# Moving the softmax division of a local-attention kernel from ScalarE to VectorE

## The chip, the cores and the metric

The kernel runs on one core of a Trainium2 chip. The metric is the device time of one execution in microseconds, from the first to the last instruction with the small launch share around them; lower is better. The engines are PE (TensorE, matrix products and transposes), ACT (ScalarE), DVE (VectorE), POOL (GpSimd) and SP (SyncE, which issues the DMAs here). Each has a queue of its own and works it off strictly in order; they meet at semaphores.

## The reference

The input is `x` of 2 sequences x 2048 tokens x 512 features and a context of 2 x 154 tokens. All arithmetic is fp32. Cut to what matters:

```
x = x + cross_attention(layernorm(x), ctx, ctx)          # 16 heads
h = layernorm(x)
for l in range(2):                                        # local attention + gated FFN
    qkv = shift_token(h) @ wqkv[l]                        # 512 -> 3 x 512, 8 heads of 64
    q, k = rotary_xpos(l2norm(q) * qs, l2norm(k) * ks)
    sim  = (8 * q) @ k.T                                  # query block of 256, keys of it and the block before
    sim  = where(mask, -max, sim)                         # query i sees keys i-256 .. i
    attn = softmax(sim)                                   # exp(sim - max) / sum
    h    = h + (attn @ v) @ wo[l]
    z    = layernorm(shift_token(h)) * g + b
    a, g = split(z @ w1 + b1);  h = h + (a * gelu(g)) @ w2 + b2
out = x + h
```

## The kernel before

The 4096 tokens are 32 tiles of 128 (`NT = 32`). The phases follow one another: context and cross attention, then twice (for `l` 0 and 1) an attention phase and an FFN phase. Every fp32 product is made of three fp32r products (`split_matmul`, L46 to L48), of a rounded high part, which ACT writes (`hi_...`), and a remainder, which DVE writes (`lo_...`).

`attention_phase` is the function that the change touches. Each engine runs a hand-written order over the tiles `t`, pipelined so that projections run for tile `t + 2`, rotary and key work for `t + 1`, and softmax and values for `t`. A tile has 8 heads in two halves of four (`LANES = 4`). For one head: PE writes scores to PSUM (`scores`, L1246), DVE adds the mask and finds the maximum (`masked`, L1477, out `neg_s`, `neg_m`), ACT takes the exponential with a running sum (`exponent`, L1365, out `prob`, `sm`), DVE inverts the sums of two heads at a time (`recip`, L1486, out `rc`), and ACT multiplies `prob` in place by `rc` (`divide`, L1374). PE then transposes `prob` (`transpose_p`, L1258) into the PSUM bank of the head four further on, so it also waits until `masked` has read that bank. ACT and DVE split the transposed probabilities (`hi_p` L1380, `lo_p` L1491), PE multiplies with `v` (`values`), ACT and DVE split the result (`hi_o` L1390, `lo_o` L1501), and PE applies `wo` (`output`). A full tile sees 384 keys, the first two tiles of each sequence 128 and 256.

Beside it go the norms of q and k. ACT squares the projection (`squares`, L1338), DVE sums it and clamps it (`norms`, L1446 and L1448), POOL takes the root as a power (L1156, `rn`), DVE scales (`normalise`, L1454, `qk`), and POOL applies the rotary tables in four instructions: one with the cosines (L1162), two halves with the sines (L1168), and their sum (L1172, `m`). `a = 0` is q and `a = 1` is k. PE transposes `m` (L1227). `lo_v` (L1461), `lo_h` (L1440) and `residual` (L1510) are further DVE steps of one instruction each; `project(t + 2, 0)` on PE waits for `lo_h(t + 2)`, and `hi_v` (L1344) on ACT precedes `lo_v`.

At the end of the phase DVE also prepares the first FFN group: `ffn_moments` (L1614 to L1620) and `ffn_normalise` (L1632), with a root on POOL between them (L1626).

Of the kernel before, what the change touches and what calls it, by code (L numbers as in the profile page):

```python
# [9 lines left out]
ACT = mybir.ActivationFunctionType  # L10
# [939 lines left out]
def attention_sems(sem):  # L950

    s = {n: [sem(f"a_{n}{u}") for u in range(4)] for n in ("ld_h", "ld_rot", "ld_y", "st")}
    for n in ("ld_small", "k_copy", "dv_own", "pe_h", "ac_h", "dv_h", "pe_qkv", "ac_sq", "dv_ssq", "pl_rn", "dv_norm",
              "pl_tab", "pl_m1", "pl_m2", "pl_rot", "ac_v", "dv_v", "pe_r", "ac_r", "dv_r", "pe_s", "dv_s", "ac_exp", "dv_rc", "ac_p",
              "pe_t", "ac_t", "dv_t", "pe_o", "ac_o", "dv_o", "pe_w", "dv_y"):
        s[n] = sem(f"a_{n}")
    s["w_ld"], s["w_hi"], s["w_lo"] = [sem(f"w_attn_ld{k}") for k in range(SLOTS["w_attn"])], sem("w_attn_hi"), sem("w_attn_lo")
    return s
# [16 lines left out]
def attention_phase(nc, io, ps, ident, s, neg_half, l, h_in, y_in, w, dram, ahead):  # L975
    LH = NT * HEADS

    with ExitStack() as st:
# [38 lines left out]
        def nth(total, n):  # L1017

            return l * total + max(n, 0)
# [5 lines left out]
        def seen(t):  # L1025
            return slice(first_block(t) * P, KEYS)
# [31 lines left out]
        with nc.Block() as block:  # L1058
# [131 lines left out]
            def _(e):  # L1190
# [60 lines left out]

                def transpose_p(t, h):
                    n = HEADS * t + h
                    e.wait_ge(s["ac_p"], nth(LH, n + 1))

                    e.wait_ge(s["dv_s"], nth(LH, min(n + LANES + 1, LH)))
                    for k in range(first_block(t), 3):
                        last = e.transpose(ps[:, bank_head(h), k * P:(k + 1) * P], prob[:, n % 4, k * P:(k + 1) * P], ident[:])  # L1258
                    last.then_inc(s["pe_t"], 1)
# [16 lines left out]
                def output(t):  # L1276
                    if t < 0:
                        return
                    if t == 0:
                        e.wait_ge(w_lo, w.done(w.count))  # L1280
                    e.wait_ge(s["dv_o"], nth(2 * NT, 2 * t + 2))

                    e.wait_ge(s["dv_r"], nth(2 * NT, min(2 * t + 6, 2 * NT)))
                    for c in range(DC):
                        last = split_matmul(e, ps[:, bank_y(t), :], [x[:, t % 2, c, :] for x in oT], [x[:, c, :] for x in wo], c == 0, c == DC - 1)
                    last.then_inc(s["pe_w"], 1)
# [10 lines left out]
                for t in range(NT):  # L1297
                    if t:
                        scores(t, 1)
                    project(t + 1, 2)  # L1300
                    transpose_h(t + 2)
                    if t == 0:
                        scores(t, 1)
                    for h in range(LANES):
                        transpose_p(t, h)
                    transpose_qk(t + 1)
                    project(t + 2, 0)
                    for h in range(LANES):
                        values(t, h)

                    scores(t + 1, 0)
                    project(t + 2, 1)
                    if t == NT - 1:
                        output(t - 1)
                    for h in range(LANES, HEADS):
                        transpose_p(t, h)
                    if t < NT - 1:
                        output(t - 1)
                    for h in range(LANES, HEADS):
                        values(t, h)  # L1320
                output(NT - 1)
# [2 lines left out]
            def _(e):  # L1324
# [34 lines left out]
                def exponent(t, h):  # L1359
                    if t < NT:  # L1360
                        n = HEADS * t + h
                        m = n % 4
                        e.wait_ge(s["dv_s"], nth(LH, n + 1))
                        e.wait_ge(s["pe_t"], nth(LH, n - 3))
                        e.activation(prob[:, m, seen(t)], neg_s[:, m, seen(t)], ACT.Exp, bias=neg_m[:, m:m + 1], scale=-1.0,  # L1365
                                     accum_out=sm[:, m:m + 1]).then_inc(s["ac_exp"], 1)

                def divide(t, p):

                    if t < NT:  # L1370
                        n = HEADS * t + 2 * p
                        e.wait_ge(s["dv_rc"], nth(LH // 2, n // 2 + 1))
                        for m in (n % 4, n % 4 + 1):
                            e.activation(prob[:, m, seen(t)], prob[:, m, seen(t)], ACT.Copy, scale=rc[:, m:m + 1]).then_inc(s["ac_p"], 1)  # L1374

                def hi_p(t, h):
                    n = HEADS * t + h
# [24 lines left out]
                squares(1, 1)  # L1402
                for h in range(LANES):
                    exponent(0, h)
                divide(0, 0)
                divide(0, 1)
                for t in range(NT):
                    hi_o(t - 1, 1)
                    hi_v(t + 1)
                    hi_h(t + 2)  # L1410
                    for h in range(LANES):
                        hi_p(t, h)
                    hi_qk(t + 1)
                    for h in range(LANES, HEADS):
                        exponent(t, h)
                    divide(t, 2)
                    squares(t + 2, 0)
                    divide(t, 3)

                    hi_o(t, 0)  # L1420
                    squares(t + 2, 1)
                    for h in range(LANES, HEADS):
                        hi_p(t, h)
                    for h in range(LANES):
                        exponent(t + 1, h)
                    divide(t + 1, 0)
                    divide(t + 1, 1)
                hi_o(NT - 1, 1)

            @block.vector  # L1430
            def _(e):
# [18 lines left out]
                def normalise(t, a):  # L1450
                    if t < NT:
                        e.wait_ge(s["pl_rn"], nth(2 * NT, 2 * t + a + 1))
                        e.wait_ge(s["pl_rot"], nth(2 * NT, 2 * t + a - 1))
                        e.tensor_tensor(token_major_heads(qk[:, a, :]), token_major_heads(ps[:, bank_qkv(t, a), :]),  # L1454
                                        rn[:, a, :].rearrange("p (h o) -> p h o", o=1).to_broadcast([P, HEADS, DH]),
                                        ALU.mult).then_inc(s["dv_norm"], 1)
# [7 lines left out]
                def lo_qk(t):  # L1464
                    if t < NT:
                        for a in range(2):
                            e.wait_ge(s["ac_r"], nth(2 * NT, 2 * t + a + 1))
                            hi, out = ((qT[x][:, t % 2] if a == 0 else kT[x][:, :, 2 + t % 4, :]) for x in range(2))
                            e.tensor_tensor(out, ps[:, bank_r(t, a), :].rearrange("p (c t) -> p c t", c=DC), hi.bitcast(F32),
                                            ALU.subtract).then_inc(s["dv_r"], 1)  # L1470
# [7 lines left out]
                                               scalar=3.0e38, op0=ALU.add, op1=ALU.min, accum_out=neg_m[:, n % 4:n % 4 + 1]  # L1478
                                               ).then_inc(s["dv_s"], 1)

                def recip(t, p):

                    if t < NT:
                        n = HEADS * t + 2 * p
                        e.wait_ge(s["ac_exp"], nth(LH, n + 2))
                        e.reciprocal(rc[:, n % 4:n % 4 + 2], sm[:, n % 4:n % 4 + 2]).then_inc(s["dv_rc"], 1)  # L1486

                def lo_p(t, h):
                    n = HEADS * t + h
# [36 lines left out]
                norms(1, 1)  # L1526
                for h in range(LANES):
                    masked(0, h)
                recip(0, 0)
                recip(0, 1)  # L1530
                normalise(1, 1)
                for t in range(NT):
                    for h in range(LANES, HEADS):
                        masked(t, h)
                    lo_o(t - 1, 1)
                    residual(t - 2)
                    lo_v(t + 1)
                    lo_h(t + 2)
                    for h in range(LANES):
                        lo_p(t, h)  # L1540
                    lo_qk(t + 1)
                    if t == NT - 1:
                        ffn_normalise(e, ahead["s"], ahead["t"], l, 0)
                    recip(t, 2)
                    recip(t, 3)
                    norms(t + 2, 0)

                    for h in range(LANES):
                        masked(t + 1, h)
                    lo_o(t, 0)  # L1550
                    normalise(t + 2, 0)
                    norms(t + 2, 1)
                    for h in range(LANES, HEADS):
                        lo_p(t, h)
                    recip(t + 1, 0)
                    recip(t + 1, 1)
                    normalise(t + 2, 1)
                    if t == NT - 2:
                        ffn_moments(e, ahead["s"], ahead["t"], l, 0)
                residual(NT - 2)  # L1560
                lo_o(NT - 1, 1)
                residual(NT - 1)
# [443 lines left out]
```

## Time and profile before

| | |
|---|---|
| device time, 3 runs | 3564.11 us median (3563.64 to 3566.64) |
| profiled execution, device time | 3564.11 us |
| its span, first to last instruction | 3562.3 us |
| PE, DVE, ACT, POOL busy | 96%, 55%, 48%, 32% of the span |
| attention phases | about 600 to 1320 us and 2100 to 2820 us of the span |

The busy shares are means over phases that differ. DVE, ACT and POOL are most busy in the two attention phases and much less in the FFN phases; PE is busy nearly throughout. Matmuls are pipelined and overlap in the rows, so the distance between the starts of two of them is less than the duration of one. The same holds for the other engines, where an instruction's row begins a little before the one ahead of it ends.

### The profile page before, as it was taken

The numbers are of one execution on the slowest core, as the hardware profiler recorded it, in microseconds if no ns is written. First come the engines' busy times: TensorE is split into PE (matmuls) and PEld (weight loads), VectorE is DVE, ScalarE is ACT, GpSimd is POOL, SyncE is SP. The second block draws the span as 40 slices with busy tenths as digits, with TensorE's granted clock in tenths as the row PEclk, the third lists the DMA queues.
The fourth block names the chain that finished last, engine by engine and source line by source line (L and its number), as shares of the span: only waits on it lengthen the run. The fifth ranks groups of instructions, "written<-read, shape, count | busy, mean of one in ns | idle before, by whom it ended". The sixth has DMA issues, their size and how long they took to land. (4 is left out here: it accounts for less than half of the span.)

```text
span 3562.3 us, 56374 instructions
## 1 busy us (share of the span) xinstructions
PE 3412.7 (96%) x20560; PEld 2797.1 (79%) x20560; DVE 1955.5 (55%) x4484; ACT 1702.7 (48%) x4490; POOL 1133.0 (32%) x1008
## 2 busy tenths in 40 slices
PE   7999996999999989999999979999999899999999
PEld 5666675888888877888888858888888778888887
DVE  6888875677777764223323247776777643233322
ACT  5666663677777763111111137777777521111111
POOL 3434433555555520000000035555555121101111
PEclk9999998999999999999999989999999999999999
DMA  4112213111221122111111111112111331111111
GB/s 123 42 46 65 72 42 125 37 60 60 65 67 61 61 87 83 44 44 43 43 44 44 64 65 51 61 61 65 64 60 58 120 100 49 36 46 50 45 37 38
DMA packets 186869, 216.26 MB, mean 61 GB/s; under 512 B 27094, under 2 KB 125654, under 8 KB 186595
## 3 DMA queue, kind: packets, MB, share of 16 engines
q1 hardware_dynamic: 186595, 212.65, 18.6%
q8 instruction: 166, 2.72, 0.3%
q14 instruction: 108, 0.88, 0.1%
HBM read 125.79 MB, written 69.00 MB: 55 GB/s over the span
## 5 line engine op out<-in xcount | busy, mean ns | idle before, releaser
L1917 DVE SCALAR_TENSOR_TENSOR u_full<-banks,b_cols,gate 128x512 f32<-128x512 f32 (+1 forms) x176 | 132.1, 750 | 877.2 <-ACT gate L1875 803.8
L1875 ACT ACTIVATE gate<-banks,b_cols 128x512 f32<-128x512 f32 (+1 forms) x176 | 121.3, 689 | 1008.3 <-PE banks L48 1008.3
L46 PE MATMUL banks<-fxT_h,w_h 128*128 128x512 f32 (+1 forms) x1408 | 556.7, 395 | 2.6 <-DVE w_l L1901 2.4
L48 PE MATMUL banks<-fxT_h,w_l 128*128 128x512 f32 (+1 forms) x1408 | 556.9, 395 | 0.0
L47 PE MATMUL banks<-fxT_l,w_h 128*128 128x512 f32 (+1 forms) x1408 | 555.9, 395 | 0.0
L1770 POOL TENSOR_TENSOR sums<-sums,b_rows 128x512 f32<-128x512 f32 x64 | 85.5, 1368 | 878.7 <-DMA sums<-z_rows 878.7
L46 PE MATMUL banks<-wqkv_h,hT_h 128*128 128x512 f32 x768 | 325.7, 424 | 15.8 <-DVE wqkv_l L1435 14.4
L46 PEld LDWEIGHTS banks<-fxT_h,w_h 128*128 128x128 f32 (+1 forms) x1408 | 260.2, 185 | 70.3 <-DVE w_l L1901 3.7
L48 PEld LDWEIGHTS banks<-fxT_h,w_l 128*128 128x128 f32 (+1 forms) x1408 | 260.8, 185 | 67.4
L47 PEld LDWEIGHTS banks<-fxT_l,w_h 128*128 128x128 f32 (+1 forms) x1408 | 260.5, 185 | 67.1
L48 PE MATMUL banks<-wqkv_h,hT_l 128*128 128x512 f32 x768 | 305.0, 397 | 0.0
L47 PE MATMUL banks<-wqkv_l,hT_h 128*128 128x512 f32 x768 | 304.9, 397 | 0.0
L1365 ACT ACTIVATE prob<-neg_s,neg_m 128x384 f32<-128x384 f32 (+2 forms) x512 | 302.5, 629 | 3.4 <-DVE neg_m L1477 3.4
L1374 ACT ACTIVATE prob<-prob,rc 128x384 f32<-128x384 f32 (+2 forms) x512 | 273.3, 613 | 7.5 <-DVE rc L1486 7.5
L46 PE MATMUL banks<-pT_h,v_h 128*64 128x128 f32 x1440 | 265.1, 223 | 11.3 <-DVE pT_l L1491 11.3
L48 PE MATMUL banks<-pT_h,v_l 128*64 128x128 f32 x1440 | 264.7, 222 | 0.0
L47 PE MATMUL banks<-pT_l,v_h 128*64 128x128 f32 x1440 | 264.6, 222 | 0.0
L1477 DVE CUSTOM_DVE_ANT_0 neg_s<-banks,mask 128x384 f32<-128x384 f32 (+2 forms) x512 | 242.2, 529 | 24.9 <-PE banks L1246 24.2
L1156 POOL TENSOR_TENSOR rn<-ssq,neg_half 128x8 f32<-128x8 f32 x128 | 211.8, 1655 | 130.8 <-DVE ssq L1448 130.6
L46 PE MATMUL banks<-w_h,u_h 128*128 128x512 f32 x640 | 251.8, 393 | 0.5 <-DVE u_l L1922 0.5
L47 PE MATMUL banks<-w_l,u_h 128*128 128x512 f32 x640 | 250.6, 392 | 0.0
L48 PE MATMUL banks<-w_h,u_l 128*128 128x512 f32 x640 | 249.0, 389 | 0.0
(190 smaller groups left out, 8095.3 us busy)
## 6 DMA issues: line engine op xcount, KB each, us to landing
y_rows<-sums SPq DMA_DIRECT2D x16, 1024.0 KB
sums<-y_rows SPq DMA_DIRECT2D x64, 256.0 KB, 2.9
z_rows<-sums SPq DMA_DIRECT2D x64, 256.0 KB, 2.0
sums<-z_rows SPq DMA_DIRECT2D x16, 1024.0 KB, 5.6
thirds<-in_w SPq DMA_DIRECT2D x30, 512.0 KB, 4.9
thirds<-in_x SPq DMA_DIRECT2D x8, 1024.0 KB, 6.9
x_rows<-thirds SPq DMA_DIRECT2D x8, 1024.0 KB, 4.3
thirds<-y_rows SPq DMA_DIRECT2D x64, 128.0 KB, 2.8
```

The source lines that it names most:

```text
L46: pe.matmul(out, a_h, b_h, start=start, stop=False)
L47: pe.matmul(out, a_h, b_l, start=False, stop=False)
L48: return pe.matmul(out, a_l, b_h, start=False, stop=stop)
L1156: e.tensor_tensor(rn[:, a, :], ssq[:, a, :], neg_half[:, 0:HEADS], ALU.pow).then_inc(s["pl_rn"], 1)
L1365: e.activation(prob[:, m, seen(t)], neg_s[:, m, seen(t)], ACT.Exp, bias=neg_m[:, m:m + 1], scale=-1.0, accum_out=sm[:, m:m + 1]).then_inc( ...
L1374: e.activation(prob[:, m, seen(t)], prob[:, m, seen(t)], ACT.Copy, scale=rc[:, m:m + 1]).then_inc(s["ac_p"], 1)
L1477: e.tensor_tensor_reduce(out=neg_s[:, n % 4, seen(t)], in0=ps[:, bank_head(h), seen(t)], in1=mask[:, seen(t)], scale=-1.0, scalar=3.0e38, ...
L1770: e.tensor_tensor(res[:, tt, :], res[:, tt, :], b2[:], ALU.add).then_inc(s["pl_b2" if ends else "pl_res"], 1)
L1875: e.activation(gate[r, :], ps[r, 2 * (m % 2) + 1, :], ACT.Gelu, bias=b1[r, place[m], 1:2]).then_inc(s["ac_g"], 1)
L1917: e.scalar_tensor_tensor(out=u_full[r, m % 2, :], in0=ps[r, 2 * (m % 2), :], scalar=b1[r, place[m], 0:1], in1=gate[r, :], op0=ALU.add, op1 ...
```

## The change

The multiplication of `prob` by `rc` moves from ACT (`activation` with a scale) to DVE (`tensor_scalar` in place). DVE's `recip` becomes `divide`: the reciprocal, a wait on its own semaphore, and two multiplications. The semaphore `ac_p` becomes `dv_p`, and `exponent` also waits for the division of the same lane's last head. The orders of DVE, ACT and, in the last tile, PE are rewritten: on DVE `lo_o(t - 1, 1)` comes ahead of `masked(t, 4..7)`, `norms(t + 2, 0)` stands between the two divisions of the second half, and `normalise(t + 2, 1)` now stands ahead of the divisions of `t + 1`; on ACT `squares(t + 2, 0)` stands in the middle of the four exponentials; `ffn_moments` and `ffn_normalise` move by about a tile.

```diff
@@ tensor queue @@
-                    e.wait_ge(s["ac_p"], nth(LH, n + 1))
+                    e.wait_ge(s["dv_p"], nth(LH, n + 1))
...
-                    if t == NT - 1:
-                        output(t - 1)
                     for h in range(LANES, HEADS):
                         transpose_p(t, h)
-                    if t < NT - 1:
-                        output(t - 1)
+                    output(t - 1)
@@ scalar queue @@
+                        e.wait_ge(s["dv_p"], nth(LH, n - 3))
...
-                def divide(t, p):
-                    if t < NT:
-                        n = HEADS * t + 2 * p
-                        e.wait_ge(s["dv_rc"], nth(LH // 2, n // 2 + 1))
-                        for m in (n % 4, n % 4 + 1):
-                            e.activation(prob[:, m, seen(t)], prob[:, m, seen(t)], ACT.Copy, scale=rc[:, m:m + 1]).then_inc(s["ac_p"], 1)
...
-                    for h in range(LANES, HEADS):
-                        exponent(t, h)
-                    divide(t, 2)
+                    exponent(t, 4)
+                    exponent(t, 5)
                     squares(t + 2, 0)
-                    divide(t, 3)
+                    exponent(t, 6)
+                    exponent(t, 7)
...
-                    divide(t + 1, 0)
-                    divide(t + 1, 1)
@@ vector queue @@
-                def recip(t, p):
+                def divide(t, p):
                     if t < NT:
                         n = HEADS * t + 2 * p
                         e.wait_ge(s["ac_exp"], nth(LH, n + 2))
                         e.reciprocal(rc[:, n % 4:n % 4 + 2], sm[:, n % 4:n % 4 + 2]).then_inc(s["dv_rc"], 1)
+                        e.wait_ge(s["dv_rc"], nth(LH // 2, n // 2 + 1))
+                        for m in (n % 4, n % 4 + 1):
+                            e.tensor_scalar(prob[:, m, seen(t)], prob[:, m, seen(t)], rc[:, m:m + 1], None, ALU.mult).then_inc(s["dv_p"], 1)
...
                 for t in range(NT):
+                    lo_o(t - 1, 1)
                     for h in range(LANES, HEADS):
                         masked(t, h)
-                    lo_o(t - 1, 1)
                     residual(t - 2)
                     lo_v(t + 1)
                     lo_h(t + 2)
                     for h in range(LANES):
                         lo_p(t, h)
                     lo_qk(t + 1)
+                    divide(t, 2)
+                    norms(t + 2, 0)
+                    divide(t, 3)
                     if t == NT - 1:
-                        ffn_normalise(e, ahead["s"], ahead["t"], l, 0)
-                    recip(t, 2)
-                    recip(t, 3)
-                    norms(t + 2, 0)
-
+                        ffn_moments(e, ahead["s"], ahead["t"], l, 0)
+
+                    lo_o(t, 0)
+                    normalise(t + 2, 0)
                     for h in range(LANES):
                         masked(t + 1, h)
-                    lo_o(t, 0)
-                    normalise(t + 2, 0)
                     norms(t + 2, 1)
                     for h in range(LANES, HEADS):
                         lo_p(t, h)
-                    recip(t + 1, 0)
-                    recip(t + 1, 1)
                     normalise(t + 2, 1)
-                    if t == NT - 2:
-                        ffn_moments(e, ahead["s"], ahead["t"], l, 0)
+                    divide(t + 1, 0)
+                    divide(t + 1, 1)
+                    if t == NT - 1:
+                        ffn_normalise(e, ahead["s"], ahead["t"], l, 0)
```

## Rows read from the trace of the kernel before

**Rows 1.** The page: busy time, share of the span, instructions.
```profile
PE 3412.7 (96%) x20560; PEld 2797.1 (79%) x20560; DVE 1955.5 (55%) x4484; ACT 1702.7 (48%) x4490; POOL 1133.0 (32%) x1008
```

**Rows 2.** Windows, one tile: stretch, PE, PEld, DVE, ACT, POOL busy, clock, DMA.
```profile
819.20:841.42 22.22, 22.22 (x183) 19.33 (x182) 15.95 (x44) 16.25 (x43) 11.94 (x11) 1.00 0.16 49
```

**Rows 3.** Waits of PE in the first attention phase: us, times, longest.
```profile
PE banks L46 <- DVE pT_l L1491: 5.7, 4, 1.7
...
PE banks L1258 <- DVE neg_m L1477: 2.1, 2, 1.6
```

**Rows 4.** Timeline of DVE in that tile: start, us, line, tiles, idle before.
```profile
820.04 0.56 DVE L1477 CUSTOM_DVE_ANT_0 neg_s<-banks,mask 128x384 f32<-128x384 f32 x1 [0.38 <-PE banks L1246]
...
821.95 0.84 DVE L1501 TENSOR_TENSOR oT_l<-banks,oT_h 64x256 fp32r<-64x256 f32 x2
822.83 0.69 DVE L1510 TENSOR_TENSOR sums<-banks,sums 128x512 f32<-128x512 f32 x1
...
824.77 0.68 DVE L1440 TENSOR_TENSOR hT_l<-banks,hT_h 128x512 fp32r<-128x512 f32 x1
825.37 1.94 DVE L1491 TENSOR_TENSOR pT_l<-banks,pT_h 128x384 fp32r<-128x384 f32 x4
...
836.64 0.17 DVE L1448 TENSOR_SCALAR ssq<-ssq 128x8 f32<-128x8 f32 x1
836.72 1.94 DVE L1491 TENSOR_TENSOR pT_l<-banks,pT_h 128x384 fp32r<-128x384 f32 x4
838.63 0.17 DVE L1486 RECIPROCAL rc<-sm 128x2 f32<-128x2 f32 x1
...
841.19 0.69 DVE L1454 TENSOR_TENSOR qk<-banks,rn 128x512 f32<-128x512 f32 x1 [1.21 <-POOL rn L1156]
```

**Rows 5.** Timeline of POOL, from that tile into the next.
```profile
836.66 1.45 POOL L1168 TENSOR_TENSOR m<-qk,rot 128x256 f32<-128x256 f32 x2
...
841.96 1.29 POOL L1162 TENSOR_TENSOR m<-qk,rot 128x512 f32<-128x512 f32 x1 [0.81 <-DVE qk L1454]
843.20 1.44 POOL L1168 TENSOR_TENSOR m<-qk,rot 128x256 f32<-128x256 f32 x2
844.78 1.30 POOL L1172 TENSOR_TENSOR m<-m 128x512 f32<-128x512 f32 x1
```

**Rows 6.** Timeline of PE in that tile.
```profile
825.87 0.48 PE L46 MATMUL banks<-wqkv_h,hT_h 128*128 128x512 f32 x1
...
830.80 0.22 PE L48 MATMUL banks<-pT_h,v_l 128*64 128x128 f32 x1
```

**Rows 7.** Timeline of ACT in that tile.
```profile
831.85 0.80 ACT L1390 ACTIVATE oT_h<-banks 64x256 fp32r<-64x256 f32 x2
```

**Rows 8.** Groups by line and shape: busy us, mean ns, idle before.
```profile
L1477 DVE CUSTOM_DVE_ANT_0 neg_s<-banks,mask 128x384 f32<-128x384 f32 x448 | 223.0, 554 | 20.0 <-PE banks L1246 19.7
...
L1156 POOL TENSOR_TENSOR rn<-ssq,neg_half 128x8 f32<-128x8 f32 x128 | 211.8, 1655 | 130.8 <-DVE ssq L1448 130.6
...
L1632 DVE TENSOR_SCALAR thirds<-thirds,f_mv,f_rs 128x512 f32<-128x512 f32 x64 | 30.6, 543 | 15.9 <-POOL f_rs L1626 15.9
```

**Rows 9.** One line's instructions in one window: ns min/median/max, first start.
```profile
L833 DVE TENSOR_SCALAR xn<-thirds,x_mv,x_rs x1: 1082/1082/1082, 121.7 to 121.7; 128x512 f32<-128x512 f32 x1
```

**Rows 10.** Timelines of POOL and DVE at 121 us and 597 us.
```profile
121.28 1.21 POOL L575 TENSOR_TENSOR x_prob<-x_prob,x_rc 128x616 f32<-128x616 f32 x1 [0.66 <-DVE x_rc L857]
...
597.40 0.76 DVE L1448 TENSOR_SCALAR ssq<-ssq 128x8 f32<-128x8 f32 x1
...
598.68 1.22 DVE L1435 TENSOR_TENSOR wo_l<-thirds,wo_h 128x512 fp32r<-128x512 f32 x1
...
596.86 1.28 POOL L1162 TENSOR_TENSOR m<-qk,rot 128x512 f32<-128x512 f32 x1 [2.20 <-DVE qk L1454]
598.09 1.25 POOL L1168 TENSOR_TENSOR m<-qk,rot 128x256 f32<-128x256 f32 x1
```

**Rows 11.** Timeline of PE at the end of the first attention phase.
```profile
1302.33 1.95 PE L1258 MATMUL banks<-ident,prob 128*128 128x128 f32 x12 [1.55 <-DVE neg_m L1477]
```

More of the change, by code:

```diff
@@ L953, in attention_sems @@
     for n in ("ld_small", "k_copy", "dv_own", "pe_h", "ac_h", "dv_h", "pe_qkv", "ac_sq", "dv_ssq", "pl_rn", "dv_norm",
-              "pl_tab", "pl_m1", "pl_m2", "pl_rot", "ac_v", "dv_v", "pe_r", "ac_r", "dv_r", "pe_s", "dv_s", "ac_exp", "dv_rc", "ac_p",
+              "pl_tab", "pl_m1", "pl_m2", "pl_rot", "ac_v", "dv_v", "pe_r", "ac_r", "dv_r", "pe_s", "dv_s", "ac_exp", "dv_rc", "dv_p",
               "pe_t", "ac_t", "dv_t", "pe_o", "ac_o", "dv_o", "pe_w", "dv_y"):
@@ L1404, in _ @@
                     exponent(0, h)
-                divide(0, 0)
-                divide(0, 1)
                 for t in range(NT):
@@ L1528, in _ @@
                     masked(0, h)
-                recip(0, 0)
-                recip(0, 1)
                 normalise(1, 1)
+                divide(0, 0)
+                divide(0, 1)
                 for t in range(NT):
+                    lo_o(t - 1, 1)
                     for h in range(LANES, HEADS):
                         masked(t, h)
-                    lo_o(t - 1, 1)
                     residual(t - 2)
```

## The prediction

> **What bounds the kernel now.** I read the page first, for the shares of the engines [rows 1]: PE is busy 96% of the span and DVE, ACT and POOL have room on average. The change lies in the two attention phases, so I then took the windows of one tile there [rows 2]. A full tile takes 22.22 us, PE is busy for all of it at a granted clock of 1.00, DVE for 15.95 us and ACT for 16.25 us. The timelines of the next tiles show the same starts plus 22.22 us. So PE sets the pace. Its waits in a whole attention phase are a few at the ends [rows 3]. Taking work off ACT, which waits for PE, can gain nothing in a full tile; the question is whether DVE, with more to do, begins to hold PE up. For that I read the timelines of the four engines in the tile that starts at 819.20 us [rows 4 to 7], and last the groups and the places where DVE and POOL want something at once [rows 8 to 10].
>
> **What the change costs on DVE.** The nearest row to the new multiplication is L1632, the same instruction with 512 columns and two per-partition scalars: 543 ns [rows 8]. If it took one column per cycle of 0.96 GHz, its 512 columns alone would be 533 ns and leave 10 ns for everything else, while 8 columns (L1448) cost 170 ns [rows 4]. So it takes two columns at a time. With 384 columns it is 67 ns shorter, 476 ns, with one scalar too many; from the other side 170 ns plus 188 columns (98 cycles x 2) make about 370 ns. I take 410 ns, and 330 ns from start to start (rows on DVE overlap by 80 ns [rows 4]). A pair also needs its reciprocal and the wait for it, about 190 ns. Eight heads: 8 x 0.33 + 4 x 0.1 = 3.0 us more per tile. 15.95 + 3.0 = 19.0 us, still under 22.22. ACT loses eight instructions, which nobody behind them on the path needed sooner.
>
> **Where it stands in time.** DVE's order now puts the divisions of heads 0 to 3 behind `normalise(t + 2, 1)`, which waits for a root on POOL and in turn starts POOL's four rotary instructions. Behind the divisions stand `lo_o`, four `masked`, `residual`, `lo_v` and `lo_h`, and for `lo_h` PE waits in `project(t + 2, 0)`, which starts at 825.87, 6.67 us into the tile [rows 6]. From the end of the divisions to `lo_h`: 0.87 (`lo_o`, 821.95 to 822.83), 1.91 (`masked`, 820.04 to 821.95), 0.60 and 0.61 for two instructions of 512 columns, 0.68 and a semaphore of 0.05 for `lo_h` [rows 4]: 4.72 us. DVE must be free of divisions at 6.67 - 4.72 = 1.95 us into the next tile, which begins at 841.42.
>
> Without any conflict it is: `normalise` could start at 839.3 (root done), the two pairs follow at 839.9 and take 2 x 0.85 us, until 841.6, which is 0.2 us into the tile. That leaves 1.75 us of cover.
>
> **The conflict with POOL.** DVE's two-column instructions and POOL's instructions exclude each other. At 597.40 the small L1448 meets POOL's L1162 and takes 0.76 us instead of 0.17; it ends at 598.16, and POOL's ended at 598.14 [rows 10]. At 121.7 L833 (512 columns, two scalars, alone 0.54 us) takes 1.082 us and ends at 122.77, 0.28 us behind the end of POOL's instruction at 122.49 [rows 9, 10]. So a DVE instruction that meets a running POOL one ends 0.02 us plus its columns behind it: 0.22 us for 384. A POOL instruction waits likewise: the half with the sines that starts at 598.09 beside a DVE instruction takes 1.25 us, not 0.72, and DVE's next one, at 598.68, waits for it and takes 1.22 us [rows 10]. They alternate; neither gets two turns in a row. POOL's 0.72 us after a wait is 0.58.
>
> Now the chain, with PE on its old times. PE's values end at 831.02 [rows 6], ACT's `hi_o` needs 0.80 [rows 7], `lo_o` on DVE 0.87, so `normalise(t + 2, 0)` starts at 832.76. POOL starts 0.77 us later (841.19 to 841.96) and reaches its sum 2.82 us after that (to 844.78) [rows 4, 5]: the sum runs from 836.35 to 837.65. The clamp L1448 comes at 836.64 as before, in the middle of it, and waits: DVE goes on at 837.59, not 836.72. Four `lo_p` take 1.91, so `normalise(t + 2, 1)` starts at 839.50; the root is ready (837.67 + 1.66 [rows 8] = 839.33). Then:
> - 840.10 reciprocal, 840.29 division 0; POOL's L1162 starts at 840.27 and ends at 841.55; division 0 ends at 841.77.
> - POOL's first half runs then, to 842.35; division 1 ends at 842.57.
> - Reciprocal 842.49, division 2 is issued at 842.68, POOL's second half runs to 843.15; division 2 ends at 843.37.
> - Division 3 is issued at 843.29. POOL's sum is issued 0.14 to 0.15 us after the half before it (843.20 + 1.44 to 844.78 [rows 5]), at 843.30.
>
> This last is a race within 10 ns. If DVE wins, division 3 ends at 843.70, DVE is free at 843.62, 2.20 us into the tile, 0.25 us late. If POOL wins, its sum runs to 844.50, division 3 ends at 844.72, DVE is free at 844.64, 3.22 us in, 1.27 us late. The trace has a like case: at 836.64 L1448 is 0.02 us ahead of POOL's L1168 (836.66) and takes 0.17 us, no wait [rows 4, 5]. So who is issued first wins, and my times put DVE first by a hair. The loop closes through PE (`lo_h`, projection, values, `hi_o`, and the next norms), so a lateness is paid in full in each tile. `masked(t, 7)` before PE's transposes and the divided `prob` itself have more room than `lo_h`.
>
> How many tiles: 448 `masked` of 384 columns are 56 full tiles [rows 8]; the last two of each layer have no projection behind, so 52. 52 x 0.25 = 13 us; 52 x 1.27 = 66 us.
>
> **The moves at the end of the phase.** `ffn_moments` used to stand ahead of `masked(31, 4..7)`, and PE waited 1.55 us there [rows 11]; now it stands behind. Summed the same way, PE's last values start about 1 us earlier in each layer, in spite of PE's transposes no longer having `output(30)` as cover. Gain 2 us in all. `ffn_normalise` ends before the last `residual` either way.
>
> **What a page says.** The Trainium skill (Advanced Engine Details and Errata, VectorE Performance Modes) says that VectorE's second port is shared with GpSimd and that instructions in a two-port mode and GpSimd's block each other. The rows of 121 and 597 us agree, with 0.54 and 0.59 us of waiting. The skill's VectorE: DVE Perf Modes (The TRN2 errata) estimates such an instruction at 58 cycles plus half its columns, 260 ns for 384; the row of 512 columns, 543 ns against the 327 of that rule, does not bear it out. By that estimate the work added would be 2.5 us per tile and the wait for POOL the same.
>
> **The rivals.**
> - DVE loses the race in most tiles: 3564 + 66 - 2 = 3628 us. For it: POOL needs only 10 ns. Against it: the case at 836.64.
> - The waits are covered. Either the instruction takes one column at a time and does not meet POOL, when 8 of 0.47 us ([rows 4], L1491) still end 0.7 us into the tile, or DVE is elsewhere earlier by the 0.25 us that I find it late. Then only the end of the phase counts: 3562 us.
> - It gets worse than one lost race: at 476 ns a division is free 0.07 us later each time, and the tail of a waiting one can be longer by as much. Four of them add 0.28 us to 1.27: 52 x 1.55 = 81 us, 3643 us.
> - Faster. PE's waits for `lo_p` and `masked` in the first phase are 5.7 + 2.1 us [rows 3], some of them behind ACT's exponentials and divisions at the start and end of the sequences. If ACT's relief removes all, in both layers, it is 15.6 us: 3549 us. It decides only if no full tile is late; against it, most of these waits are at the end, where DVE, not ACT, is last [rows 11].
>
> **How the numbers follow.** The profiled execution, 3564.11 us, is also the median, and its span is 1.8 us less; the sum is 3564.1 + 13 - 2 = 3575 us. Chances: this case 0.36, the lost race 0.28, covered 0.19, worse 0.08, faster 0.09. The range leaves out about a tenth on each side: 3559 to 3642 us. My forecast's own range, with the lateness from 0.05 to 0.45 us, is 3565 to 3585. About 0.2%, 7 us, is what a measurement tells from no change. Faster by more: 0.09. Within it: the covered case and the part of mine with a lateness under 0.17 us, 0.26. Slower: 0.65.
>
> **What would show it.** In the profile after: L1374 gone from ACT; about 512 TENSOR_SCALAR rows on DVE, half of them (heads 4 to 7) near 0.41 us and half stretched to 0.5 to 1.5 us beside POOL's rotary rows; L1448 at 1.0 us in one of two cases; a tile of 22.47 us (23.5 if the race is lost), PE's new waits for `hT_l`, or in the worse case also `neg_m` and `v_l`; POOL's halves stretched by up to 0.1 to 0.5 us. The prediction fails if the divisions are not stretched, if `normalise(t + 2, 1)` comes at another time than 20.3 us into the tile, or if PE's wait falls on `prob` itself.

## The result, and the profile after

The changed kernel takes 3669.08 us (median of 4 runs, 3663.69 to 3672.61), the kernel before 3563.88 us in the same rounds (3562.16 to 3566.64). The ratio is 1.0293, with a 95% interval of 1.0275 to 1.0311: 105 us slower. That is 27 us above the upper end of the predicted range.

The page of the kernel after, its line of busy times:

```profile
PE 3486.1 (95%) x20560; PEld 2795.5 (76%) x20560; DVE 2329.7 (64%) x4996; ACT 1511.2 (41%) x3978; POOL 1148.0 (31%) x1008
```

Against [rows 1], ACT is busy for 191 us less and DVE for 374 us more, with 512 more instructions. At the predicted 0.41 us the 512 would be 210 us. The groups by line and shape of the kernel after (busy us, mean ns, idle before) show the rest:

```profile
L1475 DVE TENSOR_SCALAR prob<-prob,rc 128x384 f32<-128x384 f32 x448 | 332.9, 783 | 7.9
...
L1434 DVE TENSOR_SCALAR ssq<-ssq 128x8 f32<-128x8 f32 x128 | 66.9, 523 | 4.4
```

A division takes 783 ns in the mean, nearly twice what it takes alone, and the eight-column clamp, 0.17 us when alone [rows 4], takes 523 ns.

The window of one full tile, in the columns of [rows 2]:

```profile
834.00:857.53 23.53, 23.36 (x182) 19.25 (x181) 21.45 (x52) 13.17 (x34) 11.99 (x12) 1.00 0.15 47
```

The tile has grown from 22.22 to 23.53 us. PE is still busy for nearly all of it at a clock of 1.00, so neither the share of PE nor the clock tells what happened. The timeline of DVE around the start of this tile, with divisions 0 and 2 also on a row of their own:

```profile
829.21 1.02 DVE L1434 TENSOR_SCALAR ssq<-ssq 128x8 f32<-128x8 f32 x1
830.14 1.94 DVE L1480 TENSOR_TENSOR pT_l<-banks,pT_h 128x384 fp32r<-128x384 f32 x4
832.00 0.68 DVE L1440 TENSOR_TENSOR qk<-banks,rn 128x512 f32<-128x512 f32 x1
...
832.79 1.48 DVE L1475 TENSOR_SCALAR prob<-prob,rc 128x384 f32<-128x384 f32 x1
832.79 2.29 DVE L1475 TENSOR_SCALAR prob<-prob,rc 128x384 f32<-128x384 f32 x2
...
835.19 0.70 DVE L1475 TENSOR_SCALAR prob<-prob,rc 128x384 f32<-128x384 f32 x1
835.19 2.13 DVE L1475 TENSOR_SCALAR prob<-prob,rc 128x384 f32<-128x384 f32 x2
837.24 0.84 DVE L1490 TENSOR_TENSOR oT_l<-banks,oT_h 64x256 fp32r<-64x256 f32 x2
```

And POOL's timeline over the same time:

```profile
832.76 1.28 POOL L1162 TENSOR_TENSOR m<-qk,rot 128x512 f32<-128x512 f32 x1 [0.80 <-DVE qk L1440]
834.00 1.67 POOL L1168 TENSOR_TENSOR m<-qk,rot 128x256 f32<-128x256 f32 x2
835.81 1.29 POOL L1172 TENSOR_TENSOR m<-m 128x512 f32<-128x512 f32 x1
```

Read the ends. POOL's L1162 ends at 834.04 and division 0 at 834.27. The four divisions of one tile take 1.48, 0.89, 0.70 and 1.51 us, in turn with POOL's four instructions. POOL's sum starts at 835.81 and ends at 837.10; division 3 starts at 835.81 too and ends 0.22 us behind it, at 837.32. It waited for the whole sum. So DVE is free at 837.24, 3.24 us into the tile.

The timeline of PE:

```profile
838.83 1.96 PE L1258 MATMUL banks<-ident,prob 128*128 128x128 f32 x12
840.86 1.23 PE L1227 MATMUL banks<-ident,m 128*128 128x128 f32 x8
841.96 0.50 PE L46 MATMUL banks<-wqkv_h,hT_h 128*128 128x512 f32 x1
```

`project(t + 2, 0)` starts 7.96 us into the tile (841.96 - 834.00), not 6.67 [rows 6]. The 12 transposes of `prob`, which take 1.47 us in the kernel before, take 1.96. The timeline of PE's weight loads tells why:

```profile
838.79 0.31 PEld L1258 LDWEIGHTS banks<-ident,prob 128*128 128x128 f32 x3 [0.30 <-issue]
839.27 0.31 PEld L1258 LDWEIGHTS banks<-ident,prob 128*128 128x128 f32 x3 [0.16 <-issue]
839.75 0.31 PEld L1258 LDWEIGHTS banks<-ident,prob 128*128 128x128 f32 x3 [0.17 <-issue]
```

They come in threes, one head at a time, 0.48 us apart, which is the pace of DVE's `masked`. PE runs at DVE's pace here, in gaps that the profile lists as "issue" and does not put down to DVE. It goes on like that up to `project(t + 2, 0)`:

```profile
840.83 0.42 PEld L1227 LDWEIGHTS banks<-ident,m 128*128 128x128 f32 x4 [0.29 <-issue]
841.43 0.42 PEld L1227 LDWEIGHTS banks<-ident,m 128*128 128x128 f32 x4 [0.18 <-issue]
841.96 0.19 PEld L46 LDWEIGHTS banks<-wqkv_h,hT_h 128*128 128x128 f32 x1
```

DVE's `residual` ends at 840.71 and PE goes on at 840.83; `lo_v` ends at 841.31, PE goes on at 841.43; `lo_h` ends at 841.91 and `project` starts 0.05 us later. Behind it no step of PE's tile is later by more than these 1.3 us.

**Where the 105 us are.** `lo_v` runs once per tile, 32 times in a phase. Here is that line by source, in each attention phase of the kernel after (ns min/median/max, first and last start):

```profile
L1447 DVE TENSOR_TENSOR v_l<-banks,v_h x32: 680/681/684, 602.8 to 1339.3; 128x512 fp32r<-128x512 f32 x32
...
L1447 DVE TENSOR_TENSOR v_l<-banks,v_h x32: 679/681/692, 2148.9 to 2883.2; 128x512 fp32r<-128x512 f32 x32
```

The same line in the kernel before:

```profile
L1461 DVE TENSOR_TENSOR v_l<-banks,v_h x32: 680/692/693, 604.9 to 1286.9; 128x512 fp32r<-128x512 f32 x32
...
L1461 DVE TENSOR_TENSOR v_l<-banks,v_h x32: 680/692/693, 2096.0 to 2777.4; 128x512 fp32r<-128x512 f32 x32
```

From first to last it is 736.5 us and 734.3 us now, 682.0 and 681.4 before: 107.4 us more. (The two profiled executions differ by 106.5 us over the whole span; the first `lo_v` comes 2.1 us earlier now.) Of the 31 intervals of a phase, three stand at the start of each of its two sequences, in and next to the tiles with one or two key blocks; there the sum over both phases has grown by 30.1 us. They are called the short tiles below. The other 50 intervals have grown by 77.3 us, 1.55 us each: none is under 23.53 us, and the mean is 23.75.

### The profile page after: what moved, and what is told of

It reads as the page before. It is cut to its first block and busy times, and to the rows that moved or that the text cites. A ratio compares the mean times of both kernels' runs of the same rounds, so it can differ in the third digit from the quotient of the medians.

```text
span 3668.8 us, 56374 instructions
## 1 busy us (share of the span) xinstructions
PE 3486.1 (95%) x20560; PEld 2795.5 (76%) x20560; DVE 2329.7 (64%) x4996; ACT 1511.2 (41%) x3978; POOL 1148.0 (31%) x1008
## 5 line engine op out<-in xcount | busy, mean ns | idle before, releaser
L1475 DVE TENSOR_SCALAR prob<-prob,rc 128x384 f32<-128x384 f32 (+2 forms) x512 | 365.7, 755 | 9.1
L1258 PE MATMUL banks<-ident,prob 128*128 128x128 f32 x1440 | 216.8, 282 | 42.4 <-DVE neg_m L1463 39.2
L575 POOL TENSOR_TENSOR x_prob<-x_prob,x_rc 128x616 f32<-128x616 f32 x128 | 155.5, 1215 | 289.9 <-DVE x_rc L857 289.9
```

The source lines that it names most:

```text
L575: e.tensor_tensor(p4, p4, rc[:, (GT * c + tt) % NS, :].rearrange("p (r o) -> p r o", o=1) .to_broadcast([P, QUAD, SC]), ALU.mult).then_inc ...
L1475: e.tensor_scalar(prob[:, m, seen(t)], prob[:, m, seen(t)], rc[:, m:m + 1], None, ALU.mult).then_inc(s["dv_p"], 1)
```

## The experiments

The theories, as the expectations name them, are stated in full there. In short: the order of the divisions behind `normalise(t + 2, 1)` makes them meet POOL's rotary; the rivals are DVE's added work as such, and the new orders without any conflict.

### POOL's rotary taken almost away: e1_small_rotary, e1b_before_small_rotary

```
-  parts = [[token_major_heads(m[:, a, :]) for m in (qk, m1, m2)] ...]
+  parts = [[token_major_heads(m[:, a, :])[:, 0:1, :] for m in (qk, m1, m2)] ...]
```

The rotation of seven of the eight heads is left out, so the result is another one; the number and order of the instructions stay, but for one memset on POOL in each layer.

> The changed kernel with GpSimd's four rotary instructions cut to one head of eight; VectorE's work, order and number of instructions are those of the changed kernel (the rotation of seven heads is left out of the computation). Theory A (VectorE's divisions and its clamp wait for GpSimd's long instructions at the shared port, and that alone makes VectorE late): full tiles fall back to 22.2 us, divisions to about 0.41 us each, time 3555 to 3572 us. Rival B (3 us more of work per tile on VectorE, queued behind normalise, is enough by itself): tiles stay at 23.5 to 23.8 us and the time near 3669 us. Between them, say 3600 to 3640, both have a share.

> The control: the kernel before with the same cut of GpSimd's rotary instructions (rotation of seven heads left out). TensorE sets the pace of full tiles there, so they stay at 22.22 us; the starts of the phases and sequences, where TensorE waits for the rotated keys, get shorter by some us. Theory A and B both: 3545 to 3564 us. The difference between this and the run above is what the division costs on VectorE with the port conflict gone: A says under 10 us, B about 100 us.

Measured: 3544.53 us (ratio 0.994, 0.992 to 0.996) for the kernel after with the cut, 3524.30 us (0.9883, 0.9863 to 0.9903) for the kernel before with it. Both are below the range expected, by 10 and 21 us: the short tiles got shorter than thought, by 33.3 us in the second. The window of a full tile of the first:

```profile
819.20:841.42 22.22, 22.22 (x183) 19.34 (x181) 18.91 (x51) 12.57 (x35) 6.53 (x11) 1.00 0.32 96
```

DVE is busy 18.91 us in a tile, the divisions among it, and the tile is back at 22.22 us. DVE's added work as such costs a full tile nothing; POOL's instructions beside it do. But the two kernels are 20.2 us apart, where under 10 was expected. That rest is not in full tiles: by the starts of `lo_v`, 15.2 us of it are in the short tiles. PE's waits for `masked` in the whole kernel after with the cut, and then in the kernel before with it:

```profile
PE banks L1260 <- DVE neg_m L1465: 15.1, 7, 3.7
```

```profile
PE banks L1260 <- DVE neg_m L1479: 4.3, 4, 1.6
```

The seven waits are in the short tiles and at the ends of the phases. So there is a second cost, which does not need POOL's long rotary instructions.

### Divisions ahead of normalise: e2_divide_first

```
-                    normalise(t + 2, 1)
                     divide(t + 1, 0)
                     divide(t + 1, 1)
+                    normalise(t + 2, 1)
```

> The changed kernel with the divisions of heads 0 to 3 put ahead of normalise(t + 2, 1) instead of behind it; the same instructions otherwise. Theory A: the divisions then fall in GpSimd's root instruction, which does not keep the port, and not beside its rotary instructions; TensorE's pace is back, full tiles 22.2 us, time 3560 to 3575 us. Rival B (amount of work on VectorE, wherever it stands): 3640 us or more. Rival C (a wait of GpSimd or TensorE for the later normalise takes its place): 3580 to 3640 us, with TensorE waiting for GpSimd's m.

Measured: 3573.60 us against 3565.83 (ratio 1.0021, 1.0011 to 1.0031). The difference to the kernel before was 105 us and is 7.8 us, by the move of one line in the loop and the same ahead of it. DVE's timeline:

```profile
836.69 1.03 DVE L1434 TENSOR_SCALAR ssq<-ssq 128x8 f32<-128x8 f32 x1
837.63 1.94 DVE L1480 TENSOR_TENSOR pT_l<-banks,pT_h 128x384 fp32r<-128x384 f32 x4
839.49 0.15 DVE L1472 RECIPROCAL rc<-sm 128x2 f32<-128x2 f32 x1
839.68 0.75 DVE L1475 TENSOR_SCALAR prob<-prob,rc 128x384 f32<-128x384 f32 x2
...
840.53 0.75 DVE L1475 TENSOR_SCALAR prob<-prob,rc 128x384 f32<-128x384 f32 x2
```

The pairs take 0.75 us, in a stretch in which POOL has nothing: its root ends at 839.45 and L1162 starts at 841.96 (the expectation had them inside the root). The clamp still waits (1.03 us) and costs a full tile nothing: all full tiles are 22.22 us again, and the short tiles have 5.3 us over the kernel before, not 30.1. PE waits for `masked` 6 times, 14.6 us in all, where in the kernel before it is 4 times and 4.3 us; its waits for `m` and `lo_p` have got shorter by 9.1 us.

### The race given to DVE: e5_gap

```
+                        if a == 1:
+                            e.memset(gap[:], 0.0)
                         e.tensor_tensor(y1, y1, y2, ALU.add)
```

The memset is of one column, on POOL; the instruction behind it is the sum.

> The changed kernel with one very small memset on GpSimd ahead of the sum that ends the rotary work of k, 64 in all. If the fourth division loses the port to that sum only by a race within some 10 ns, the small instruction lets it go first: the fourth division shrinks from 1.5 to about 0.4 us, a full tile from 23.6 to 22.5 or 22.6 us, and the time from 3669 to about 3615 us (52 tiles x 1.0 us). If the fourth division would lose anyway, or if the lateness is made elsewhere, the time stays within 5 us of 3669.

Measured: 3614.64 us (ratio 1.0136, 1.0116 to 1.0157). DVE's second pair:

```profile
852.52 1.03 DVE L1478 TENSOR_SCALAR prob<-prob,rc 128x384 f32<-128x384 f32 x2
```

And POOL's timeline:

```profile
853.12 0.13 POOL L1174 MEMSET gap<- 128x1 f32 x1
853.18 1.52 POOL L1175 TENSOR_TENSOR m<-m 128x512 f32<-128x512 f32 x1
```

With 0.06 us more on POOL before its sum, division 3 is first, and POOL's sum waits instead (1.52 for 1.29 us). The pair takes 1.03 us, not 2.13. Full tiles are 22.45 to 23.67 us, 38 of the 50 under 22.7, and 22.67 in the mean, 1.08 less than in the changed kernel. More work on POOL makes the kernel 54.4 us faster: that is the price of the lost race.

### DVE divides in the old orders, ACT in the new: e3_dve_old_order, e4_order_only

The first puts back all orders of the kernel before and has DVE multiply where its reciprocals stood. The second keeps the new orders and gives the multiplication back to ACT, behind the four exponentials of each half:

```
 # e3: vector queue, order of before       # e4: scalar queue, new order
 divide(t, 2); divide(t, 3)                for h in range(LANES): exponent(t + 1, h)
 norms(t + 2, 0)                           divide(t + 1, 0)
 ...                                       divide(t + 1, 1)
 divide(t + 1, 0); divide(t + 1, 1)
 normalise(t + 2, 1)
```

> The division alone moved to VectorE, every other instruction of the three queues in the order of the kernel before (the divisions stand where the reciprocals stood, ahead of normalise(t + 2, 1)). Theory A (it is the meeting with GpSimd's rotary instructions that costs): those divisions fall before them, so full tiles stay at 22.22 us, time 3560 to 3572 us. Rival B (the added 3 us of VectorE work costs wherever it stands): 3600 us or more.

> The new orders of the three queues without the move: ScalarE divides, behind the four exponentials of each half, VectorE keeps only the reciprocals. Theory A: full tiles 22.22 us; the phase ends are about 1 us shorter each because ffn_moments stands behind the last masked: 3558 to 3566 us. Rival D (the new order, above all normalise ahead of the reciprocals, is what costs): 3600 us or more, since ScalarE then waits for the reciprocals behind the root on GpSimd.

Measured: 3565.99 us against 3567.28 for e3 (ratio 0.9998, 0.9989 to 1.0007), no change that can be told. For e4 3647.52 us (1.023, 1.0216 to 1.0244): my theory expected no more than 3566 and missed; the rival that the orders cost by themselves held. By the timelines its cause is another chain. ACT's timeline in e4:

```profile
852.32 2.14 ACT L1370 ACTIVATE prob<-prob,rc 128x384 f32<-128x384 f32 x4 [1.12 <-DVE rc L1484]
854.36 0.76 ACT L1386 ACTIVATE oT_h<-banks 64x256 fp32r<-64x256 f32 x2
```

DVE's timeline behind it:

```profile
855.15 0.85 DVE L1499 TENSOR_TENSOR oT_l<-banks,oT_h 64x256 fp32r<-64x256 f32 x2 [2.81 <-ACT oT_h L1386]
856.03 0.56 DVE L1475 CUSTOM_DVE_ANT_0 neg_s<-banks,mask 128x384 f32<-128x384 f32 x1
```

The reciprocals stand behind `normalise`, so ACT's four divisions begin late; `hi_o` comes behind them, `lo_o` waits 2.81 us for it, and `masked` stands behind `lo_o`. No division meets POOL there, and the tile is 23.33 us all the same. So e4 does not separate the orders from the conflict in the changed kernel, where `hi_o` has no such delay; e3 and e2 do.

### The source split in three rows: e6_one_port

```
-  e.tensor_scalar(prob[:, m, seen(t)], prob[:, m, seen(t)], rc[:, m:m + 1], None, ALU.mult)
+  e.tensor_scalar(prob[:, m, seen(t)], prob[:, m, seen(t)].rearrange("p (a k) -> p a k", a=3), ...)
```

This is done for the full tiles only.

> The changed kernel, same order and same result, but for full tiles the division's source is written as 3 x 128 columns and its destination as 384, so that source and destination have unlike shapes; meant to make VectorE take one column per cycle. If that works, the slower instruction is alone at one port and never waits for GpSimd. Theory A (the port): division rows all near 0.50 us instead of 0.41 or 0.8 to 1.5, VectorE free of divisions some 0.8 us into the next tile, full tiles back at 22.2 us, time 3566 to 3582 us, although the instruction by itself is slower. Rival B (work on VectorE): slower than 3669 us, by up to 64 x 8 x 0.1 = 50 us. If the shapes make no difference to the hardware, all stays at 3669 us.

Measured: 3674.08 us (ratio 1.0305, 1.029 to 1.0321), a division 781 ns in the mean. No difference, and none could come: the trace records the source of these instructions as one run of 384, as in the changed kernel, so the three rows that touch had been joined before VectorE saw them. The run tells nothing about the ports.

### The source in three rows that don't touch: e9_unlike_shapes

```
-        neg_s = sb("neg_s", [P, 4, KEYS])
+        neg_s = sb("neg_s", [P, 4, 3, P + 4])
...
-  e.tensor_scalar(prob[:, m, seen(t)], prob[:, m, seen(t)], rc[:, m:m + 1], None, ALU.mult)
+  e.tensor_scalar(prob[:, m, seen(t)], neg_s[:, m, first_block(t):3, 0:P], rc[:, m:m + 1], None, ALU.mult)
```

Beside this, `masked` writes the three blocks, and the exponential is taken in place in `neg_s`; so the division no longer works in place, and `masked` also waits for the division that last read its block.

> The changed kernel, same order and result, with neg_s laid out as three blocks of 128 columns that are 132 apart (the exponential is taken in place there) and the division writing from it to a contiguous prob of 384. Writing the shapes alone differently changed nothing (3674 us, 781 ns per division), so this time they are really unlike: an odd outer count of 3 at the source, one even run of 384 at the destination. If VectorE then takes one column per cycle, the division should be near 0.50 to 0.55 us, with no stretching beside GpSimd's rotary rows. Theory A (waiting for GpSimd is what costs): VectorE is free of divisions some 0.8 us into the next tile, full tiles are 22.2 us, time 3566 to 3585 us, although the instruction alone is slower. Rival B (work on VectorE): 3669 us or up to 50 us more. If the divisions still take 0.41 us alone and 0.8 to 1.5 us beside GpSimd, they still use both ports and the time stays at 3665 to 3680 us.

Measured: 3589.72 us against 3566.59 (ratio 1.0068, 1.0052 to 1.0085), 5 us above the range expected; the division is slower than the 0.50 to 0.55 us expected. DVE's timeline:

```profile
839.73 1.25 DVE L1435 TENSOR_SCALAR ssq<-ssq 128x8 f32<-128x8 f32 x1
...
843.54 1.13 DVE L1479 TENSOR_SCALAR prob<-neg_s,rc 128x384 f32<-128x384 f32 x2
...
844.78 1.13 DVE L1479 TENSOR_SCALAR prob<-neg_s,rc 128x384 f32<-128x384 f32 x2
```

And POOL's, over the same time:

```profile
843.51 1.28 POOL L1162 TENSOR_TENSOR m<-qk,rot 128x512 f32<-128x512 f32 x1 [0.81 <-DVE qk L1441]
844.76 1.41 POOL L1168 TENSOR_TENSOR m<-qk,rot 128x256 f32<-128x256 f32 x2
```

Both pairs lie beside POOL's instructions and neither side waits. All 448 divisions of 384 columns take 0.60 to 0.62 us. By itself the division is slower here: 1.13 us for a pair, not 0.75. The kernel is 79 us faster than the changed one, and its full tiles are 22.22 us in the mean; of the 23 us that it has over the kernel before, 20.9 are in the short tiles. The clamp, left as it was, still waits (1.25 us).

This is the run that shows the exclusion to be a matter of the form of DVE's instruction, and not of DVE and POOL as such. The other things that it changes are not the reason: in the tiles with two key blocks the source is in `neg_s` too, in two rows that don't touch, and there the division takes what it takes in the changed kernel. First e9, then the changed kernel, all divisions of 256 columns:

```profile
L1479 DVE TENSOR_SCALAR prob<-neg_s,rc 128x256 f32<-128x256 f32 x32 | 17.1, 576 | 0.6
```

```profile
L1475 DVE TENSOR_SCALAR prob<-prob,rc 128x256 f32<-128x256 f32 x32 | 17.1, 576 | 0.6
```

In both, 12 of the 32 are held up, to as much as 1.42 us. The Trainium skill (VectorE: DVE Perf Modes, What auto-detection actually checks) says that the two-port mode wants a single source and a destination in SBUF with outermost dimensions both even or equal; the source of three rows before a destination of one run is neither. The trace agrees: undisturbed divisions of 128, 256 and 384 columns take 0.29, 0.35 and 0.42 us in the changed kernel (the first of a pair), so all but the columns is about 0.22 us. The 384 columns then take 0.20 us there and 0.39 here, twice as long.

### masked ahead of lo_o, with the divisions in either place: e7_masked_first, e8_masked_first_divide_last

```
                 for t in range(NT):
-                    lo_o(t - 1, 1)
                     for h in range(LANES, HEADS):
                         masked(t, h)
+                    lo_o(t - 1, 1)
```

Both do this, and the same in the other half of the tile. e7 also has the edit of e2; e8 has not.

> Divisions of heads 0 to 3 ahead of normalise(t + 2, 1), and masked again ahead of lo_o in both halves of a tile; what is left of the new order is the place of the clamp between the divisions and of the FFN preparation. The run with the divisions first alone was 3573.6 us, with TensorE waiting 3.9 us for neg_m at the short tiles of the second sequence and 2.2 us at the end. If those waits come from masked standing behind lo_o, which waits for TensorE's values through ScalarE, they go: 3562 to 3569 us. If not, 3572 to 3576 us.

> The changed kernel with only masked put ahead of lo_o again, the divisions still behind normalise(t + 2, 1). Then lo_o(t, 0) and normalise(t + 2, 0) are late by four masked, 1.9 us, GpSimd's work on q ends 1.7 us later, so the root for k and normalise(t + 2, 1) too, and with it the divisions and their meeting with GpSimd. By the sum of rows a full tile is late by 1.27 + 1.7 = about 3.0 us, less what the clamp saves: 24.5 to 25.3 us per tile, time 3690 to 3740 us. If masked behind lo_o is what costs in full tiles, it would be faster than 3669 us instead.

Measured: 3566.23 us against 3562.54 for e7 (ratio 1.0008, 0.9999 to 1.0017), 3.7 us over its kernel before where e2 was 7.8 us over, and the longest wait for `masked` (3.9 us in e2) is gone. The gain is not in the short tiles, which are 258.0 us in all and 258.4 in e2, but at the ends of the phases: from the last `lo_v` to the start of the last `output` it is 30.1 us, and 32.8 to 32.9 in e2. e8 is 3756.38 us (1.0535, 1.0517 to 1.0552), 16 us above what was expected. Its full tiles are 25.20 us and more, 25.27 as the median. PE's waits in e8 (us, times, longest):

```profile
PE banks L1258 <- DVE neg_m L1463: 74.5, 64, 3.6
PE banks L1227 <- DVE sums L1499: 54.1, 58, 1.1
```

Here `lo_o` and the norms behind it come later, so the root and the conflict do too, and `masked` now stands right behind the stretched divisions. e7 and e8 differ only in the place of two divisions against one `normalise`, and that is 190 us. No version tried that computes the same is faster than the kernel before; e3 and e7 can't be told from it.

## Why the prediction was wrong

**Right.** PE sets the pace and the lateness is paid in each tile. DVE's added instructions cost a full tile nothing where they don't meet POOL (e1, e2, e3). The size of one: 0.41 us alone and 0.33 from start to start; e2's pair takes 0.75. The exclusion and its tail of 0.22 us, the strict alternation, the clamp's wait to 1.02 us. My chain for the lost race gives 1.48, 0.89, 0.69 and 1.43 us for the four divisions; measured are 1.48, 0.89, 0.70 and 1.51. It puts `project(t + 2, 0)` at 7.94 us; measured is 7.96. The tile for that case was given as 23.5 us, and the shortest are 23.53. That the chain comes out within 0.02 us is in part luck: `normalise` starts 2.00 us before the next tile where the chain had 1.92, and POOL's sum takes 1.29 us where it had 1.20. One of the prediction's own signs of failing, `normalise(t + 2, 1)` at another time than 20.3 us into the tile, came true (21.53), but only because the tile is by then 1.31 us late; counted from the next tile it is in its place.

**The step that failed.** "My times put DVE first by a hair." The chain had division 3 issued at 843.29 and POOL's sum at 843.30, took the one case in the trace where DVE was 0.02 us ahead as the rule, and made DVE's win the forecast. POOL wins, in every full tile that has such a meeting, 54 in all: division 3 takes 1.5 us in each. e5 prices this step at 54.4 us; the prediction had 52 x 1.02 = 53 us between its two cases. The sum of terms each known to 10 or 20 ns can't order two events 10 ns apart, so the lost race should have had at least as much chance as the won one. The order was in fact as forecast, as far as rows can tell it: in the trace's own ns, division 3's row starts 0.001 to 0.009 us ahead of the sum's in all 54, and loses. So what failed is the prediction's "who is issued first wins", taken down to 0.01 us. The row of 836.64 [rows 4, 5] shows it for 0.02 us; in e5 the lead is 0.036 to 0.042 us and DVE wins every time; under 0.01 us it does not hold.

**What was mis-sized.** The rival of the lost race gave 3628 us, and the time is 3669. Two terms were missing or short.
- Short tiles, 30.1 us, were taken as nothing. The prediction counted 52 full tiles and left out the starts of the sequences. Over the kernel before, the short tiles of e2 have 5.3 us: so some 25 of the 30.1 come with the divisions' place behind `normalise(t + 2, 1)`. About half of the 30.1 does not need POOL's long rotary instructions: it is 15.2 us in e1 against e1b (and 20.9 in e9, where only the divisions of full tiles are free of POOL). That short tiles have too little work on PE to cover DVE's wait for POOL's root is argued from this, not shown. `masked` behind `lo_o`, which e7 puts back, is no part of the 30.1; it costs 4.1 us (each against its own runs of the kernel before) to 7.4 us (directly) at the ends of the phases.
- The full tiles cost 1.55 us each, not 1.27. The shortest are at 1.31 over before. In the longer ones POOL's scaling of the tables (L1148, released by the transfer of `rot`), which the prediction did not consider, runs later, beside the division pair of heads 6 and 7, ahead of the root that `normalise(t + 2, 0)` waits for. DVE and then POOL in the tile that starts one `lo_v` at 745.25 and the next at 769.64, 24.39 us:

```profile
751.70 1.23 DVE L1475 TENSOR_SCALAR prob<-prob,rc 128x384 f32<-128x384 f32 x2
```

```profile
751.88 0.84 POOL L1148 TENSOR_TENSOR rot<-rot,qk_scale 128x256 f32<-128x256 f32 x1 [10.16 <-DMA rot<-in_rot]
752.79 1.65 POOL L1156 TENSOR_TENSOR rn<-ssq,neg_half 128x8 f32<-128x8 f32 x1
```

The clamp was done at 751.23 and the root starts 1.56 us behind it. `normalise(t + 2, 0)` starts 9.22 us behind `lo_v`, where it is 8.23 in the shortest tiles, and this tile is 0.86 us longer than they are. The tiles sort by it without exception: in 23 of the 50 the scaling starts 4.24 to 5.71 us behind `lo_v`, and they take 23.53 to 23.62 us; in the other 27 it starts at 5.78 to 6.89, and they take 23.67 to 24.70. No run took the scaling away by itself. With the race won (e5), the lateness is 0.23 us at the least, where 0.25 was predicted, and 0.45 in the mean, by the same scaling.

**The gain at the end of the phase** was put at 1 us for each layer. The measured stretch from the last `lo_v` of a phase to the first of the next is 809.1 us before (2096.0 - 1286.9) and 809.6 after (2148.9 - 1339.3): no gain. Of it, the last `output` starts 30.4 us behind the last `lo_v` in both phases before, and 32.3 and 31.1 us after: PE's last steps come later, not earlier.

**Who waits.** PE's new waits were predicted for `hT_l`, and in the worse case also for `neg_m` and `v_l`. That is how they come in the tile shown: for each `masked`, for `residual`, for `lo_v`, and the last for `lo_h`, 0.05 us behind which `project(t + 2, 0)` starts. The profile's table of waits names only the first, and only where the gap is long enough:

```profile
PE banks L1258 <- DVE neg_m L1463: 39.2, 47, 4.5
```

**The rivals.** "Covered" falls with the stretched divisions; "faster" with the full tiles. "Worse than one lost race" named 3643 us for a slower division; the time is even higher, but for the reasons above and not for that one, since the division was sized rightly.

## What to carry to other kernels

A multiplication moved from ScalarE to VectorE cost nothing that could be measured (e3), and the same multiplication a few lines further down cost most of 105 us: 77 in full tiles, because there it ran beside GpSimd, and most of the rest in the short tiles at a loop's start, about half of it without GpSimd's long instructions. Before moving a one-source fp32 instruction to VectorE, lay its new place over GpSimd's timeline, and put it where GpSimd waits for VectorE anyway. Where it can't be moved, a slower form that takes one column at a time can be the faster one. Where a chain worked out from rows ends in two events closer than the rows' own resolution, give both outcomes their chance, and take the short tiles at the start and end of a loop as a term of their own.

## What the runs showed of the hardware

- The exclusion is between single instructions, in turn, and the loser waits for the whole of the winner. A lag of under 0.01 us (both start at 835.81 in the rows) decides over 1.1 us.
- It hangs on the form of the addresses: 448 divisions with a source of three rows that don't touch were not held up beside POOL (e9); with two such rows, or one run, they were. An instruction of 8 columns waits as well as one of 384 (1.02 us for 0.17). And it is not only the one-source form that waits: L1435, with both sources in SBUF, took 1.22 us beside POOL [rows 10] and 0.69 alone, at 593.4 to 595.5.
- POOL's root does not take part. In the kernel after, DVE's pair of divisions inside it takes its undisturbed 0.75 us; DVE's row and then POOL's:

```profile
823.51 0.75 DVE L1475 TENSOR_SCALAR prob<-prob,rc 128x384 f32<-128x384 f32 x2
```

```profile
823.38 1.65 POOL L1156 TENSOR_TENSOR rn<-ssq,neg_half 128x8 f32<-128x8 f32 x1 [0.17 <-DVE ssq L1434]
```
